# A fused attention and patch-filter kernel: the last projection as a three-product fp32r split issued later, three depthwise taps on TensorE for two blocks, and a second depthwise accumulator

## What is computed

```
t  = w_in (384x384) applied to every pixel of groupnorm(x)
t  = irfft2(rfft2(t in 8x8 patches) * fft_filter)          # per channel
t  = conv2d(t, w_dw, 3x3, one kernel per channel, padding SAME)
x1, x2 = t[:192], t[192:]
g  = gelu(x1) * x2                                          # 192 channels
x  = x + w_out (384x192) applied to every pixel of g
```

## Time and profile before

| | |
|---|---|
| median of three runs | 4020.65 us |
| span of the profiled execution, first to last instruction | 4023.8 us |
| PE busy | 3617.9 us, 90% |
| DVE busy | 3421.6 us, 85% |
| ACT busy | 1368.3 us, 34% |
| POOL busy | 1436.5 us, 36% |
| mean granted TensorE clock | 0.950 |

### The profile page before, as it was taken

The page is one execution under the profiler, slowest core; times in us unless marked ns, Lnnn a source line. Parts: engine busy times, 40 slices in busy tenths (PEclk is TensorE's granted clock), DMA queues, the critical chain, the costliest instruction groups (busy, mean ns, idle before and its releaser), DMA issues.

```text
span 4023.8 us, 60589 instructions
## 1 busy us (share of the span) xinstructions
PE 3617.9 (90%) x17488; PEld 2941.8 (73%) x17488; DVE 3421.6 (85%) x5124; ACT 1368.3 (34%) x2293; POOL 1436.5 (36%) x793
## 2 busy tenths in 40 slices
PE   5988999889998899988999889997899979999898
PEld 5976679666796667966589665896659966598665
DVE  7987999779897798977989779897798878988788
ACT  2323434234332343423433233331433314333142
POOL 2542235421354123551235411454115442155411
PEclk9999999899998999989999899998999989999899
DMA  5213231233212232123221323213222132221422
GB/s 198 71 57 125 94 111 55 71 110 109 96 55 86 102 110 88 63 86 110 94 103 47 107 90 110 88 47 121 85 100 88 55 126 87 94 95 39 141 71 102
DMA packets 186256, 370.98 MB, mean 92 GB/s; under 512 B 7946, under 2 KB 9010, under 8 KB 185778
## 3 DMA queue, kind: packets, MB, share of 16 engines
q1 hardware_dynamic: 186034, 368.26, 26.6%
HBM read 267.56 MB, written 100.66 MB: 92 GB/s over the span
## 4 chain that ended last, share of the span: by engine, by line
issue 54%; POOL 22%; PE 12%; DVE 8%; ACT 2%; POOLq 1%; DMA 1%; DVEq 0%; ACTq 0%; SPq 0%
POOL x_lo L415 11%; POOL t L422 9%; POOL qn L459 2%; PE bank L1058 2%; DVE nrm L793 2%; PE bank L1078 2%; PE bank L1079 2%; DVE qt_lo L808 2%; PE bank L1083 1%; PE bank L967 1%; DVE bn_x L854 1%; ACT qt_hi L552 1%; DVE acc L888 1%; PE bank L1127 0%; POOL qn L452 0%
## 5 line engine op out<-in xcount | busy, mean ns | idle before, releaser
L415 POOL TENSOR_TENSOR x_lo<-xa,x_hi 128x512 fp32r<-128x512 f32 x363 | 547.2, 1522 | 1493.5 <-ACT x_hi L504 1493.5
L888 DVE SCALAR_TENSOR_TENSOR acc<-big,wdw,acc 128x512 f32<-128x512 f32 x1280 | 955.6, 808 | 15.9 <-ACT big L566 13.5
L980 PE MATMUL bank<-w_lo,x_hi 128*128 128x384 f32 x2322 | 795.5, 343 | 10.7 <-issue 10.7
L979 PE MATMUL bank<-w_hi,x_hi 128*128 128x384 f32 x2322 | 794.0, 342 | 4.0 <-ACT x_hi L504 4.0
L422 POOL TENSOR_TENSOR t<-t 128x768 f32<-128x768 f32 x256 | 534.1, 2087 | 731.6 <-DVE t L729 731.5
L984 PE MATMUL bank<-w_hi,x_lo 128*128 128x384 f32 x2322 | 543.9, 342 | 0.5 <-POOL x_lo L415 0.5
L739 DVE SCALAR_TENSOR_TENSOR kt<-t 128x384 f32<-128x384 f32 x256 | 530.7, 2073 | 0.0
L509 ACT ACTIVATE t<-t 128x768 f32<-128x768 f32 x256 | 217.3, 849 | 874.5 <-POOL t L422 874.5
L980 PEld LDWEIGHTS bank<-w_lo,x_hi 128*128 128x128 f32 x2322 | 444.4, 191 | 13.0 <-issue 13.0
L979 PEld LDWEIGHTS bank<-w_hi,x_hi 128*128 128x128 f32 x2322 | 445.8, 192 | 6.3 <-ACT x_hi L504 4.4
L984 PEld LDWEIGHTS bank<-w_hi,x_lo 128*128 128x128 f32 x2322 | 424.7, 191 | 1.4 <-POOL x_lo L415 1.4
(11 more groups left out here) (112 smaller groups left out, 6235.0 us busy)
## 6 DMA issues: line engine op xcount, KB each, us to landing
xr<-x SPq DMA_DIRECT2D x128, 768.0 KB, 4.7
xa<-x SPq DMA_DIRECT2D x66, 768.0 KB, 5.9
x_scratch<-xr SPq DMA_DIRECT2D x64, 768.0 KB, 3.5
xa<-x_scratch SPq DMA_DIRECT2D x64, 768.0 KB, 5.8
xr<-x_scratch SPq DMA_DIRECT2D x64, 768.0 KB, 4.7
out<-xr SPq DMA_DIRECT2D x64, 768.0 KB, 3.5
big<-x SPq DMA_DIRECT2D x8, 768.0 KB, 9.9
w_raw<-wqkv_t SPq DMA_DIRECT2D x1, 1728.0 KB, 7.0
```

Source lines behind the costliest of these rows:

```text
L415: nc.gpsimd.tensor_tensor(dst, src, hi, ALU.subtract).then_inc(s_lo, 1)
L888: nc.vector.scalar_tensor_tensor(dst, src, wdw[:, k, q:q + 1], so_far, ALU.mult, ALU.add)\
L979: nc.tensor.matmul(dst, hi(k), whi(k), start=first and k == 0, stop=False)
L980: nc.tensor.matmul(dst, hi(k), wlo(k), start=False, stop=False)
```

## The change

PE takes tap 2 of blocks 0 and 1 as well (`PE_TAPS` 3), so DVE has 20 depthwise steps instead of 22: (3,0), (3,1), (1,2), (4,0), (4,1), (2,2), (5,0), (5,1), (3,2), (4,2), (5,2) as (tap, block), and then the same nine. `acc` has two buffers. The gated product is split: ACT rounds it to `g_hi` and `g_half` (fp32r), DVE subtracts to get the rest (`gated_rest`), and `out_block` is five fp32r matmuls, four over 128 rows and one over 64. `g_half` holds the rounded last 64 channels in its lower half and their rests in its upper half.

```diff
-PE_TAPS, PE_BLOCKS = 2, 2
+PE_TAPS, PE_BLOCKS = 3, 2
...
-        wout = sb("wout", [P, 2, C])
+        wout_hi = sb("wout_hi", [P, 2, C], fp32r)
+        wout_lo = sb("wout_lo", [P, 2, C], fp32r)
+        g_hi = sb("g_hi", [P, CHUNK], fp32r)
+        g_lo = sb("g_lo", [P, CHUNK], fp32r)
+        g_half = sb("g_half", [P, CHUNK], fp32r)
...
-            [... ("acc", [P, KB, CHUNK], fp32), ...])
+            [... ("acc", [P, 2, KB, CHUNK], fp32), ...])
...
+                             (wout_raw, w_out_t)):                     # SP, at the end of the constants
-            sp.dma_start(wout[:], w_out_t).then_inc(s_late, 16)
...
+                def round_gated(c):                                   # ACT
+                    n = i * 8 + c
+                    act.wait_ge(s_out, (i * 16 + c) * 3 + 3 * (NCH + 2))
+                    act.wait_ge(s_gate, n * 2 + 5)
+                    nc.scalar.activation(g_hi[:, :], gel[:, 0], ACT.Copy).then_inc(s_rnd, 1)
+                    act.wait_ge(s_gate, n * 2 + 6)
+                    nc.scalar.activation(g_half[HD:P, :], gel[HD:P, 1], ACT.Copy)
+                    nc.scalar.activation(g_half[0:HD, :], gel[HD:P, 1], ACT.Copy).then_inc(s_rnd, 1)
...
                     if conv and edge != 1:
-                        first_tap(c - 1, KB - 1)
+                        first_tap(c - 1, KB - 1, 1 - par)
+                    if gated:
+                        round_gated(c - 2)
                     if tile:
                         copy_t(T + 2, 0)
...
             dve.wait_ge(s_cst, NCST * 16)
+            split(wout_hi[:, :, :], wout_lo[:, :, :], wout_raw, 1.0)
...
+                def gated_rest(c):                                    # DVE
+                    n = i * 8 + c
+                    dve.wait_ge(s_rnd, n * 2 + 1)
+                    nc.vector.tensor_tensor(g_lo[:, :], gel[:, 0], g_hi[:, :].bitcast(fp32), ALU.subtract).then_inc(s_rest, 1)
+                    dve.wait_ge(s_rnd, n * 2 + 2)
+                    nc.vector.tensor_tensor(g_half[HD:P, :], gel[HD:P, 1], g_half[HD:P, :].bitcast(fp32), ALU.subtract)\
+                        .then_inc(s_rest, 1)
...
-                    parts = ... else (0, 4, 8, 12, ND - 3 * KB)
+                    parts = ... else (0, 5, 7, 9, ND - 3 * KB)
                     if tile:
                         times_filter(T, 0)
-                    if within(edge, 0, NCH, -2):
-                        gate(c - 2, 0)
+                    if gated:
                         if conv:
-                            depthwise(c - 1, 0, 1)
-                        gate(c - 2, 1)
+                            depthwise(c - 1, 0, 2, 1 - par)
+                        gate(c - 2, 0, par)
+                        if conv:
+                            depthwise(c - 1, 2, 4, 1 - par)
+                        gate(c - 2, 1, par)
...
                     if tile:
                         times_filter(T + 1, 1)
                     if conv:
-                        depthwise(c - 1, parts[1], parts[2])
+                        depthwise(c - 1, parts[1], parts[2], 1 - par)
+                    if gated:
+                        gated_rest(c - 2)
                     if tile:
                         times_filter(T + 2, 0)
...
                 def out_block(c, m, tail=None):
-                    pe.wait_ge(s_gate, (i * 8 + c) * 2 + 4)
+                    pe.wait_ge(s_rest, (i * 8 + c) * 2 + 4)
...
-                    nc.tensor.matmul(dst, wout[:, 0, m * P:(m + 1) * P], gel[:, 0], start=True, stop=False)
-                    nc.tensor.matmul(dst, wout[HD:P, 1, m * P:(m + 1) * P], gel[HD:P, 1], start=False, stop=True)\
-                        .then_inc(s_out, 1)
+                    nc.tensor.matmul(dst, wout_hi[:, 0, cols], g_hi[:, :], start=True, stop=False)
+                    nc.tensor.matmul(dst, wout_lo[:, 0, cols], g_hi[:, :], start=False, stop=False)
+                    nc.tensor.matmul(dst, wout_hi[:, 0, cols], g_lo[:, :], start=False, stop=False)
+                    nc.tensor.matmul(dst, wout_hi[:, 1, cols], g_half[:, :], start=False, stop=False)
+                    nc.tensor.matmul(dst, wout_lo[0:HD, 1, cols], g_half[0:HD, :], start=False, stop=True).then_inc(s_out, 1)
...
-                    if prod:
-                        out_block(c - 2, 0, tail)
                     if tile:
                         t_tile(T + 3, m, par, 3)
                         dft_tile(T + 2, 2)
                         inverse_tile(T + 1, 1, frees=True)
                     if prod:
-                        out_block(c - 2, 1, tail)
+                        out_block(c - 2, 0, tail)
                     if tile:
                         dft_tile(T + 3, 3)
                         inverse_tile(T + 2, 2)
+                    if prod:
+                        out_block(c - 2, 1, tail)
+                    if tile:
                         inverse_tile(T + 3, 3)
...
-    nc = bacc.Bacc("TRN2", target_bir_lowering=False, num_devices=1)
+    nc = bacc.Bacc("TRN2", target_bir_lowering=False, num_devices=1, dynamic_dma_scratch_size=4096)
```

More of the change, by code:

```diff
@@ L200, in build_program @@
             [("t1", [P, 2, 2, 2, HALF], fp32), ("t2", [P, 2, 2, 2, HALF], fp32), ("kt", [P, 2, C], fp32)],
-            [("tb", [P, 2, C], fp32), ("gb", [P, 2, C], fp32), ("acc", [P, KB, CHUNK], fp32),
+            [("tb", [P, 2, C], fp32), ("gb", [P, 2, C], fp32), ("acc", [P, 2, KB, CHUNK], fp32),
              ("gel", [P, 2, CHUNK], fp32)])
+        wout_raw = w_raw[:, 2, C:3 * C].rearrange("p (a n) -> p a n", a=2)
         vt = sb("vt", [P, 2, KB, P + 1])
@@ L261, in build_program @@
         s_gate = sem("s_gate")
+        s_rnd = sem("s_rnd")
+        s_rest = sem("s_rest")
         s_past = sem("s_past")
@@ L292, in build_program @@
         TG = 2
-        NCST = 6
+        NCST = 7
         def by_patches(ap):
@@ L319, in _ @@
             sp.dma_start(w_raw[:, :, 0:C], w_in_t.rearrange("(k p) n -> p k n", p=P)).then_inc(s_raw, 16)
-            for dst, src in ((t_mats, mats), (t_gavg, gavg), (t_rowpick, rowpick), (bfc_c, bfc), (wdw, w_dw)):
+            for dst, src in ((t_mats, mats), (t_gavg, gavg), (t_rowpick, rowpick), (bfc_c, bfc), (wdw, w_dw),
+                             (wout_raw, w_out_t)):
                 sp.dma_start(dst[:], src).then_inc(s_cst, 16)
@@ L868, in _, with depthwise @@
                 ORDER = [(dy, dx) for dy in (-1, 0, 1) for dx in (-1, 0, 1)]
-                def depthwise(c, s0, s1):
+                def depthwise(c, s0, s1, par):
                     n = i * 8 + c
@@ L876, in depthwise @@
                         src = filt_img[:, k, ds(c * ROWS + (1 + dy), ROWS), 1 + dx:1 + dx + W]
-                        dst = acc[:, k].rearrange("p (r s) -> p r s", s=W)
+                        dst = acc[:, par, k].rearrange("p (r s) -> p r s", s=W)
                         before = [e for e in range(s) if DW_STEPS[e][1] == k]
@@ L889, in depthwise, with gate @@
                             .then_inc(s_dw, 1)
-                def gate(c, m):
+                def gate(c, m, par):
                     n = i * 8 + c
@@ L896, in gate @@
                     a, b = (0, 1) if m == 0 else (HD, 2)
-                    nc.vector.tensor_tensor(gel[a:P, m], gel[a:P, m], acc[a:P, b], ALU.mult).then_inc(s_gate, 1)
+                    nc.vector.tensor_tensor(gel[a:P, m], gel[a:P, m], acc[a:P, par, b], ALU.mult).then_inc(s_gate, 1)
+                def gated_rest(c):
[5 more added lines that the diff above has]
+                        .then_inc(s_rest, 1)
                 normalise(1, i * 8 + 5, 0)
@@ L910, in part_c @@
                     tile, conv = within(edge, 0, NCH), within(edge, 0, NCH, -1)
-                    parts = (0, 5, 7, 9, ND - 3 * KB) if edge == 1 else (0, 4, 8, 12, ND - 3 * KB)
+                    parts = (0, 5, 7, 9, ND - 3 * KB) if edge == 1 else (0, 5, 7, 9, ND - 3 * KB)
+                    gated = within(edge, 0, NCH, -2)
                     if tile:
                         times_filter(T, 0)
-                    if within(edge, 0, NCH, -2):
-                        gate(c - 2, 0)
+                    if gated:
                         if conv:
-                            depthwise(c - 1, 0, 1)
-                        gate(c - 2, 1)
+                            depthwise(c - 1, 0, 2, 1 - par)
[3 more added lines that the diff above has]
+                        gate(c - 2, 1, par)
                     if edge == NCH - 1:
@@ L922, in part_c @@
                     if conv and edge != 1:
-                        depthwise(c - 1, parts[0] + (1 if within(edge, 0, NCH, -2) else 0), parts[1])
+                        depthwise(c - 1, 4 if gated else parts[0], parts[1], 1 - par)
                     if tile:
@@ L930, in part_c @@
                     if conv:
-                        depthwise(c - 1, parts[2], parts[3])
+                        depthwise(c - 1, parts[2], parts[3], 1 - par)
                     if tile:
@@ L934, in part_c @@
                     if conv:
```

(8 more changed lines are left out.)

29 lines of the change are left out of this document (14 added, 15 removed).

## The result

The changed kernel takes 4113.97 us, the median of four runs (4110.56 to 4117.72). The kernel before, run four times beside it, took 4019.60 us. The ratio is 1.0233, with a 95% interval of 1.0219 to 1.0248. The change costs 94 us where I had forecast 39; the time lies above the upper end of my range, 4095. The profiled execution took 4113.15 us with a span of 4110.9, 87.1 longer than the span before. (The 87.1 is less than the 94 because the execution profiled before was one of its slower ones: span 4023.8, where the median time is 4020.65.)

The account below looks back on a forecast made before the run. PE was taken to set the step today, and a serial chain through PE and DVE after the change. +4.4 us per image, 35 for eight, plus 4 at the start gave +39: about 4060 us, range 3998 to 4095.

Parts of the forecast that it names:

- Step 0: First step of an image, ending with taps of chunk 0 and nothing to save: +1.72 us on the path.
- the start: Kernel start: splitting w_out, its earlier load and two more diagonals together cost +4 us.
- The chain of the middle step: Middle steps of part_c: taps, gates, rests and blocks in series lengthen the step from 22.28 to about 23.1 us.
- E: Start of inverse 3 on PE; from one to the next is one step, 22.28 us before the change.
- DVE's eleven instructions: DVE in a middle step, from the PSUM step of block 1 to the end of the second rest: 7.36 us.
- Step 8: Tail of an image: no tiles, held by DVE, loses only the two gate waits, -0.4 us.
- step 9: Tail of an image: rounding and last rest fit into 2.06 us, blocks get shorter, last residual comes 1.7 us earlier.
- the falling clock: Rival for six middle steps: PE's wait drops the clock for 3.4 us each, +82 us, 4140 us; chance 0.1.
- The cheap block: Rival for out_block: switching to 64 rows costs fp32r nothing, block 1.14 us, step 21.9, time 3993 us; chance 0.25.
- The waits: Rival for middle steps: DVE's chain is 0.5 to 0.8 us shorter, no change, 4020 to 4035 us; chance 0.12.
- Loads of full rows: Rival for out_block: about 0.1 us of exposed load before each of four full-row matmuls, 4120 us; chance 0.03.
- DVE's slack: DVE in the middle step: its last nine depthwise steps wait for inverse 3's image rows as before, so it has slack.

Follow-up runs that it names:

- E0: Not a run: start of inverse 3 number 0, counted from 0 within an image.
- full_rows: Changed kernel with the fifth matmul of out_block on all 128 rows instead of 64: 4056.38 us, ratio 1.0077.
- E1: Not a run: start of inverse 3 number 1, counted from 0 within an image.
- E7: Not a run: start of inverse 3 number 7, counted from 0 within an image, the last one.
- E2: Not a run: start of inverse 3 number 2, counted from 0 within an image.
- E6: Not a run: start of inverse 3 number 6, counted from 0 within an image.
- tail_filler: Changed kernel with 16 and 18 short matmuls nobody reads added where PE would wait in steps 8 and 9: 4094.67 us, ratio 1.0184.
- old_projection: Changed kernel with out_block again as two fp32 matmuls, no rounding, rests or weight split, w_out loaded late; three taps and new order stay: 4039.09 us, ratio 1.0038.
- after_no_pool: Changed kernel with POOL's low-part subtraction cut to 8 of 512 columns for chunks 2 to 7: 4114.17 us.
- gates_full_dft: Changed kernel with both gates ahead of DVE's depthwise steps, fifth matmul on 128 rows, and dft 3 ahead of out_block 0: 4046.88 us, ratio 1.0054.
- dft_no_pool: gates_full_dft with POOL's low-part subtraction cut to 8 of 512 columns for chunks 2 to 7: 3975.88 us.
- two_taps: Changed kernel with PE_TAPS back to 2, so DVE has 22 depthwise steps: 4138.56 us, ratio 1.0283.
- late_no_pool: Kernel before with out_block 0 and 1 in the later order on PE and POOL's low-part subtraction cut to 8 of 512 columns for chunks 2 to 7: 3965.74 us.

## Why the prediction was right in its direction and wrong in its size

**Step 0 and the start: right.** Step 0 grew by 20.33 - 18.61 = 1.72, the number forecast. The first inverse 3 came 4.1 later, against 4. That close a match is luck: E0 of image 0 lies between 362.5 and 364.9 in the three traces with the old start and between 365.3 and 368.7 in the ten with the new one. The means are 3.5 apart.

**The chain of the middle step: right in mechanism, short by 0.4.** I had forecast 23.1 and the mean is 23.51, in the traced step 23.55. Counted from E as in the prediction:

- Taps start at 6.10 (forecast 6.04) and are readable at 446.49 - 434.92 = 11.57 (11.4). DVE idles 0.81 ahead of them, not 1.3, because its nine depthwise steps start at E + 3.0, later than I had counted: the two ahead of the residuals, beside POOL, take 3.3 instead of 1.4.
- DVE's eleven instructions take 453.78 - 446.49 = 7.29 (7.36), and the rests are complete at 18.86 (18.8).
- PE starts `out_block` 0 at 19.15, not 18.8. This is the first term mis-sized: I had let PE start as the rest ended, and the handover of 0.29 was missing.
- From there to inverse 3 it is 458.47 - 454.07 = 4.40, not 4.26. The blocks take 1.54 and 1.52 where I had 1.42. This is the second term mis-sized, and the change of rows is not the reason: its total, 0.39, was right (`full_rows`), and the follower does pay 0.1 of it (dft 3 takes 456.36 - 455.61 = 0.75, undisturbed 0.64). I had counted five matmuls of 0.227, but the first one of a block takes 0.31 to 0.33, in `full_rows` too. Inverse 2 takes 0.59 and not 0.66, which hides a part.
- PE's waits are 0.82 and 0.87, 1.69 together, against 1.85 forecast in one place. I had seen `copy_t` 2 hold back dft 2, and that the later wait swallows it.

Over E1 to E7 the six steps cost 8.6 - 1.72 = 6.9 more per image, not 4.8: 17 us of the shortfall of 48 in the spans. The clock has a part in it. In seven of eight images it was at the lower level for 3.4 us in the step from E1 to E2, which took 23.5; in image 0, where it wasn't, 22.64. In image 0 the same happened between E6 and E7, 26.35 instead of 24.76. Together that is about 8 us.

**The tail: wrong, and this is the larger error.** The step that failed reads "Step 8 has no tiles, is held by DVE, and loses only the two gate waits: -0.4", and with it the -1.7 of step 9. Both took PE at the full clock. The tail was to be 2.1 shorter and is 1.8 longer: 3.9 per image, 31 us. The forecast of step 9's gates was good: the blocks start 563.90 - 561.73 = 2.2 after the gates end, and I had 1.9 of work in 2.06. What I missed lies ahead of it. In step 8 the rests stand behind seven depthwise steps of DVE, PE waits 3.2 to 3.9 for them, and the blocks behind the wait run at 1.2 GHz, the first in 2.70. The kernel before had a slower stretch in step 8 too, but a shorter one, behind its second block and not ahead of its first. Then DVE waits 2.04 for the residual, so that step 9's gates end 561.73 - 531.73 = 30.0 after E7 instead of 28.5, and in three images of eight the blocks of step 9 run slower once more. (That second loss hardly reaches the next image: E7 to E0 is 343.1 and 343.3 behind images 1 and 4, and 342.0 to 342.8 behind the others.) I had considered the falling clock only as a rival for the middle steps.

`tail_filler` shows the clock's share, 19.3 us. Counted to the last residual it is larger: with the clock held an image's tail ends 35.8 after E7, 1.7 earlier than in the kernel before, close to the 2.1 that I had forecast. So my terms for steps 8 and 9 hold at the full clock. The part that `tail_filler` doesn't give back lies behind the last residual, in the next image (303.4 us on average in the kernel before, 303.5 in the changed one, 304.6 here, with single values from 302.5 to 306.8 here); its cause stays open. The rope of the next image starts 4.0 later than before and not 1.8; whether that costs anything was not tested. `old_projection` shows the share of rests and clock together, 36 us.

**Rivals.** The cheap block is refuted: the change of rows costs 0.4 in this type too. (Its sign turns at a switch cost of 0.12 for the middle step, as stated, but at about 0.16 for the whole time.) The waits did not cancel. The falling clock came, but in one step of an image and not in six: about 8 us in the middle and not 82. Loads of full rows are hidden (0.23 from start to start in `full_rows`). The rule that weight loads overlap running matmuls only where the row groups differ (the Trainium skill, TensorE: Matmul & The Clock Gate, The mechanism) therefore doesn't hold here: loads into the same rows are hidden, and the one that is not is the load for 64 of them.

**DVE's slack.** That DVE "has slack" held for the changed kernel (`after_no_pool`), though for a smaller slack than I had counted. It did not hold one step on: in `gates_full_dft` my expectation failed because depthwise steps moved beside POOL (`dft_no_pool`). In `two_taps` the same is likely and not tested.

**Open.** The double-buffered accumulator alone and the scratch setting alone were not tried. Why the lower clock follows the same waits in some images and not in others isn't known.

## What to carry to other kernels

When an order is changed, walk each engine's list for instructions that others wait for and that now stand behind a wait they don't need; moving two gates was worth 62 us here. Price the edges of a pipeline as carefully as its middle: a wait on PE can also cost the clock of the matmuls behind it, here 19 us in all. And ask where an engine lands when its waits go: an instruction that is cheap where it stands can cost double beside another engine's work, as the depthwise steps did beside POOL.

## What the runs showed of the hardware that I had not expected

A matmul on 64 rows in a stream of 128-row ones costs 0.4 us more than a full one, although it does half the work (`full_rows`: 1.2 us in a step with three). The first fp32r matmul behind an fp32 one takes 0.31 to 0.33 to the next start instead of 0.23.

Depthwise steps of DVE (two inputs in SBUF, 128 x 512, fp32) take 0.68 us alone and 1.2 to 1.7 beside POOL's subtraction: in the rows above 4.74 to 4.88 for four instead of 2.73, 3.27 to 3.34 for two instead of 1.41; where they run beside POOL only in part, less. Residuals that read one input from PSUM take 1.27 to 1.28 for two in every kernel. Cutting POOL's work restores the durations in `dft_no_pool` and `late_no_pool`. The Trainium skill (SBUF — State Buffer, SBUF: two separate sides) states that DVE and GpSimd share one pair of ports as an exclusive lock, and that a DVE operation with two SBUF inputs needs it against a GpSimd operation that reads SBUF. The traces agree with that rule; it gives no duration for this case.

Waits of 3.2 to 3.9 us on PE in step 8 were followed by the 1.2 GHz level in all eight images: blocks of 2.70 us instead of 1.54. Shorter waits were followed by it too, but not each time. In image 1 these two stand just ahead of a stretch of 3.4 us at 1.2 GHz:

```profile
892.82 0.91 PE L1145 MATMUL bank<-t_mats,gb 128*128 128x128 f32 x6 [1.22 <-ACT big L573]
894.76 0.95 PE L1145 MATMUL bank<-t_mats,gb 128*128 128x128 f32 x6 [1.04 <-ACT big L573]
```

Image 0 has the same two waits, and the clock stays full behind them. Behind the waits of 0.8 us in the steps from E2 to E6 it stayed full in every image.
